# One-core MetaFormer kernel: three pairs of adder units summed on VectorE, a ring of six, and mixers, quantising and key table moved

## What is computed

```
x = x + relu(bn(adder2d_3x3(conv_3x3(relu(bn(adder2d_1x1(conv_1x1(ln(x)))))))) + ln(x))
t = t + routed(ln(t))      # 33 blocks; each takes op = argmax(h[0,0,:19]), and by two mask
                           # tables (33 x 19) for that op runs attention, a feed-forward, both or none
x = x + quantised_conv_relu x 2 (ln(x))
t = t + spectral(ln(t))    # 16 filters over the 784 tokens, mixed by 32x32 matrices
```

```
for kh in range(K):
    for kw in range(K):
        xs = xp[:, :, kh:kh + Ho, kw:kw + Wo]
        diff = jnp.abs(xs[:, None] - w[None, :, :, kh, kw, None, None])
        acc = acc - diff.sum(axis=2)          # over 32 input channels
```

## Time and profile before

| | us |
|---|---|
| runs | 362.1, 360.65, 361.57 (median 361.57) |
| profiled execution: time | 364.84 |
| profiled execution: span | 363.0 |
| PE busy in the span | 346.6 (95%) |
| DVE busy | 218.1 (60%) |
| ACT busy | 178.9 (49%) |
| POOL busy | 22.6 (6%) |
| adder 2 (first unit to last matmul) | 39.4 to 138.4 |
| first choice out | 148.2 |
| last stage | 259.8 to 359.7 |

### The profile page before, as it was taken

One profiled execution on the slowest core, in us unless ns is written; L12 is line 12 of the kernel. 1 busy time (PEld: TensorE's weight loads), 2 busy tenths in 40 slices (PEclk: granted clock), 3 DMA queues, 4 the chain that ended last, 5 costly groups with the idle time before them and its releaser, 6 DMA issues.

```text
span 363.0 us, 10721 instructions
## 1 busy us (share of the span) xinstructions
PE 346.6 (95%) x4689; PEld 208.2 (57%) x4689; DVE 218.1 (60%) x337; ACT 178.9 (49%) x182; POOL 22.6 (6%) x48
## 2 busy tenths in 40 slices
PE   8899999999999999899999998698999999999996
PEld 7436447744333335655673343384767777787873
DVE  2698999999999995454934795346422221111112
ACT  2871997878887952264827774503211111111111
POOL 5483000000000002000000000000000000000000
PEclk9999999999999999999969999969999999999999
DMA  5602800000000005400000000000140000000001
GB/s 172 223 21 57 326 13 2 2 3 2 2 2 0 2 2 206 165 5 15 1 2 2 1 3 2 7 0 0 29 110 4 4 2 4 2 4 4 2 4 46
DMA packets 12238, 13.13 MB, mean 36 GB/s; under 512 B 6027, under 2 KB 10909, under 8 KB 12185
## 3 DMA queue, kind: packets, MB, share of 16 engines
q1 hardware_dynamic: 11208, 9.17, 8.4%
q0 software_dynamic: 832, 3.00, 2.4%
q10 hardware_dynamic: 144, 0.20, 0.2%
HBM read 10.73 MB, written 0.40 MB: 31 GB/s over the span
## 4 chain that ended last, share of the span: by engine, by line
PE 64%; DVE 25%; issue 3%; ACT 2%; DMA 1%; SPq 0%; DVEq 0%; ACTq 0%
PE PS L1025 64%; DVE pool_ L848 17%; DVE pool_ L665 1%; DMA W1R<-in_fwa 1%; DVE pool_ L958 1%; DVE pool_ L845 1%; DVE pool_ L662 1%; ACT TMP L433 1%; DVE RSC L619 0%; DVE CW L783 0%; DVE CW L786 0%; DVE X L862 0%; DVE TMP L860 0%; DVE H L734 0%; DVE H L738 0%
## 5 line engine op out<-in xcount | busy, mean ns | idle before, releaser
L1025 PE MATMUL PS<-pool_,CON 128*32 128x392 f32 (+2 forms) x1320 | 111.4, 493 | 0.7 <-ACT pool_ L516 0.2
L1025 PEld LDWEIGHTS PS<-pool_,CON 128*32 128x32 f32 (+1 forms) x1320 | 48.9, 110 | 60.9 <-issue 43.8
L464 ACT ACTIVATE pool_<-TMP,WA 128x3136 f32<-128x3136 f32 x26 | 75.4, 2926 | 11.0 <-PE PS L1025 10.8
L848 DVE TENSOR_SCALAR pool_<-TMP,WA 128x3136 f32<-128x3136 f32 x44 | 79.4, 1844 | 0.1
L1003 DVE COPY pool_<-PS 128x392 f32<-128x392 f32 x32 | 18.1, 566 | 77.6 <-PE PS L1025 77.6
L565 ACT ACTIVATE pool_<-PS 128x392 f32<-128x392 f32 x32 | 15.9, 498 | 78.0 <-PE PS L1025 78.0
L1025 PE MATMUL PS<-HE,WS 128*32 128x392 f32 (+2 forms) x768 | 44.6, 386 | 0.2 <-ACT WS L557 0.2
L1025 PE MATMUL PS<-pool_,WS 128*32 128x392 f32 (+2 forms) x768 | 44.6, 385 | 0.0
L1025 PEld LDWEIGHTS PS<-pool_,WS 128*32 128x32 f32 x768 | 31.3, 109 | 12.2 <-issue 4.6
L1025 PEld LDWEIGHTS PS<-HE,WS 128*32 128x32 f32 x768 | 31.0, 110 | 12.8 <-issue 5.6
L1025 PE MATMUL PS<-CON 128*128 128x196 f32 (+1 forms) x142 | 29.9, 354 | 0.5 <-DVE QZ L652 0.5
(11 more groups left out here) (247 smaller groups left out, 334.7 us busy)
## 6 DMA issues: line engine op xcount, KB each, us to landing
pool_<-in_pho SPq DMA_DIRECT2D x1, 3144.0 KB, 11.8
HE<-in_phe SPq DMA_DIRECT2D x1, 3136.0 KB, 11.6
QZ<-CW SPq DMA_DIRECT2D x12, 98.0 KB, 2.2
CW<-in_cw POOLq DMA_DIRECT2D x2, 576.0 KB, 4.8
CON<-in_con POOLq DMA_DIRECT2D x1, 732.5 KB, 5.0
out_y<-Y SPq DMA_DIRECT2D x1, 392.0 KB, 2.4
CQ<-in_ws SPq DMA_DIRECT2D x16, 9.0 KB
MPP<-in_mpp POOLq DMA_DIRECT2D x1, 256.0 KB, 3.0
```

The source lines that it names most:

```text
L464: a.activation(unit, window(n // CQ), ACT.Abs, bias=WA2[:, n:n + 1], scale=-1.0).then_inc(s["act_unit"], 1)
L848: v.tensor_scalar(unit, window(n // CQ), WA2[:, n:n + 1], None, ALU.max).then_inc(s["dve_unit"], 1)
L1025: return t.matmul(out_, lhsT, rhs, start=start, stop=stop, skip_group_check=True)
```

## The change

- Adder 2: for c8 = 7 the units of taps (0, 1), (3, 4) and (6, 7) are summed on DVE before PE sees them: one max pass, a wait on it, then four `scalar_tensor_tensor` passes (max, add), one for each image. The pair stands in the second tap's place, the first tap's unit is gone: 69 groups instead of 72.
- The ring of adder 2 has six slots; the sixth is `QZ`, which adder 1 read and which is free by then.
- The mask tables are loaded as 19 partitions x 33. The key table is made on these (n = 16) and one DMA from SP lays it onto one partition.
- The quantising of both weights and the eight bias ops go to POOL, behind `decided`, as a chain in which each op waits for the one before: eight passes over 128 x 1152 and eight over 128 x 2. `cq_done` now comes from POOL, and the clear of `UPZ` follows it.
- `mixers(0, ...)` steps 4 and 5 move into the adder (n = 10, 12). All six of `mixers(1, ...)` move on DVE to just behind `decide(1)`. `u_mixers` move into the last stage (u = 25 to 31), and ACT's three `MUL` copies to u = 38.
- `widest`, `scales` and `box` change their n (24; 39; 20, 35, 50, 63).

```diff
 RG = 5
+RG2 = 6
+PAIRED = CQ - 1
+PAIRS = ((0, 1), (3, 4), (6, 7))
+FIRST_OF = {second: first for first, second in PAIRS}
+GROUPS = [((0,), c8) for c8 in range(CQ)]
+GROUPS += [((FIRST_OF[tap], tap) if c8 == PAIRED and tap in FIRST_OF else (tap,), c8)
+           for tap in range(9) for c8 in range(CQ) if not (c8 == PAIRED and tap in FIRST_OF.values())]
+NG = len(GROUPS)
+        def slot(g):
+            n = g % RG if g < CQ else (g - CQ) % RG2
+            return RING[:, n, :, :] if n < RG else QZ[:, :, :]
...
+            g.wait_ge(s["decided"], 1)
+            g.wait_ge(s["q_sc"], 1)
+            for src, dst, i in ((CW1, CQ1, 0), (CW2, CQ2, 1)):
+                gl(g.tensor_scalar(src[:, :], src[:, :], QS[:, 2 + i:3 + i], 1.0, ALU.mult, ALU.mult))
+                gl(g.tensor_scalar(src[:, :], src[:, :], 127.0, -128.0, ALU.min, ALU.max))
+                gl(g.tensor_scalar(src[:, :], src[:, :], 1.0, MAGIC, ALU.mult, ALU.add))
...
+                g.tensor_scalar(dst[:, :], src[:, :], -MAGIC, 1.0, ALU.add, ALU.mult).then_inc(s["cq_done"], 1)
             g.wait_ge(s["cq_done"], 2)
             g.memset(UPZ, 0.0).then_inc(s["zeroed"], 1)
...
-            for step in range(6):
+            for step in range(4):
                 mixers(0, step)
...
+                    elif len(taps) == 1:
+                        v.tensor_scalar(unit, window(taps[0]), WA2[:, at[0]:at[0] + 1], None, ALU.max).then_inc(s["dve_unit"], 1)
                     else:
-                        v.tensor_scalar(unit, window(n // CQ), WA2[:, n:n + 1], None, ALU.max).then_inc(s["dve_unit"], 1)
+                        v.tensor_scalar(unit, window(taps[0]), WA2[:, at[0]:at[0] + 1], None, ALU.max).then_inc(s["pair_half"], 1)
+                        v.wait_ge(s["pair_half"], PAIRS.index(taps) + 1)
+                        for b in range(NIMG):
+                            last = v.scalar_tensor_tensor(unit[:, b], window(taps[1])[:, b], WA2[:, at[1]:at[1] + 1], unit[:, b], ALU.max, ALU.add)
+                        last.then_inc(s["dve_unit"], 1)
...
             decide(1)
+            for step in range(6):
+                mixers(1, step)
```

More of the change, by code:

```diff
@@ L68 @@
 RG = 5
+RG2 = 6
 CQ = 8
-NG = CQ + 9 * CQ
-ON_ACT = [on_scalar(g % CQ) for g in range(NG)]
+PAIRED = CQ - 1
[5 more added lines that the diff above has]
+NG = len(GROUPS)
+ON_ACT = [on_scalar(c8) for taps, c8 in GROUPS]
 ACT_UPTO = [sum(ON_ACT[:g]) for g in range(NG + 1)]
@@ L439, in _ @@
             a.wait_ge(s["w_a_in"], 64)
-            for n in range(9 * CQ):
+            for n in range(NG - CQ):
                 g = CQ + n
+                (tap, *_), c8 = GROUPS[g]
                 if n == CQ:
@@ L445, in _ @@
                         a.activation(rows(S2P, h, 1, 1), grid(bank(4 + h)), ACT.Copy).then_inc(s["s2_ready"], 1)
[L446 to L454, removed]
                 if ON_ACT[g]:
-                    a.wait_ge(s["ring_free"], g - RG + 1)
-                    unit = RING[:, g % RG, :, :].rearrange("p b (r c) -> p b r c", r=SIDE)
+                    if n >= RG2:
+                        a.wait_ge(s["ring_free"], g - RG2 + 1)
+                    unit = slot(g).rearrange("p b (r c) -> p b r c", r=SIDE)
+                    bias = WA2[:, CQ * tap + c8:CQ * tap + c8 + 1]
                     if n == 1:
@@ L565, in _ @@
                 a.activation(UEV[:, u % 8, :], bank(u % 6), ACT.Copy).then_inc(s["uev_act"], 1)
+                if u == 38:
+                    a.wait_ge(s["u_mixed"], 4)
+                    for lag in range(3):
+                        q = slice(32 * lag, 32 * lag + 32)
+                        a.activation(MUL[q, :, :], MUS[q, :, C * lag:C * lag + C], ACT.Copy).then_inc(s["d_ready"], 1)
                 if u == 42:
@@ L776, in u_mixers @@
                                            ALU.mult, ALU.add).then_inc(s["u_mixed"], 1)
[L778 to L796, removed]
             nk = 0
@@ L804, in kl, with key_table @@
                 v.wait_ge(s["key_chain"], nk)
-            for step in range(6):
+            def key_table():
+                v.wait_ge(s["mask_in"], 32)
+                kl(v.tensor_copy(AMF[:, :], AMT[:, :]))
+                kl(v.scalar_tensor_tensor(KEY0[:, :], FMT[:, :], 2.0, AMF[:, :], ALU.mult, ALU.add))
+                kl(v.tensor_scalar(AMF[:, :], KEY0[:, :], 0.0, None, ALU.is_gt))
+                kl(v.tensor_tensor(AMF[:, :], AMF[:, :], con_("blk4", NB, NOPS), ALU.mult))
+                v.tensor_tensor(KEY0[:, :], KEY0[:, :], AMF[:, :], ALU.add).then_inc(s["key_made"], 1)
+            for step in range(4):
                 mixers(0, step)
@@ L815, in _ @@
             v.wait_ge(s["w_a_in"], 64)
-            for n in range(9 * CQ):
+            for n in range(NG - CQ):
                 g = CQ + n
-                if n == 20:
+                if n in (10, 12):
+                    mixers(0, 4 + (n - 10) // 2)
+                if n == 16:
+                    key_table()
+                if n == 24:
                     widest()
-                if n == 32:
+                if n == 39:
                     scales()
[L822 to L838, removed]
-                if not ON_ACT[g]:
-                    v.wait_ge(s["ring_free"], g - RG + 1)
-                    unit = RING[:, g % RG, :, :].rearrange("p b (r c) -> p b r c", r=SIDE)
+                if n in (20, 35, 50, 63):
+                    box((20, 35, 50, 63).index(n))
+                if not ON_ACT[g]:
+                    taps, c8 = GROUPS[g]
+                    at = [CQ * tap + c8 for tap in taps]
+                    if n >= RG2:
+                        v.wait_ge(s["ring_free"], g - RG2 + 1)
+                    unit = slot(g).rearrange("p b (r c) -> p b r c", r=SIDE)
                     if n == 0:
@@ L1117, in group @@
                     for b in range(NIMG):
-                        last = mm(PS[32 * b:32 * b + 32, 6 + h, 0:HT], SEL[ON_ACT[g]][:, g % CQ, :], half(RING[:, g % RG, b, :], h), fresh, False)
+                        last = mm(PS[32 * b:32 * b + 32, 6 + h, 0:HT], SEL[ON_ACT[g]][:, GROUPS[g][1], :], half(slot(g)[:, b, :], h), fresh, False)
                         if final and 4 * h + b < 7:
```

50 lines of the change are left out of this document (32 added, 18 removed).

## The result

The changed kernel takes 370.75 us (median of 4 runs, 368.77 to 371.19) against 361.84 for the kernel before (4 runs, 360.65 to 364.01). The ratio is 1.0229, 95% interval 1.0167 to 1.029: 2.3% slower, or 6 to 10.5 us. The forecast was 369.6. The profiled execution took 370.74, span 368.8. The profiled execution of the kernel before (span 363.0) lay 3 us above its median, so stages are compared here by landmarks and not by spans.

What follows compares the result with a forecast made beforehand. PE's pace was taken to set adder 2, with DVE only just keeping up. Adder -2.5, undisturbed mixers +0.5, taking turns +8.0 and clock +2.0 sum to +8.0 on the 361.57 median: 369.6 us, range 360.0 to 374.0.

Steps and rivals of the forecast that it cites:

- Adder, -2.5: Adder 2: three dropped groups save PE 3.95 us, less 1.5 of added waits behind the pairs, so 2.5 us gained.
- that case: Adder 2: with scalar_tensor_tensor passes of 0.97 us instead of 0.88, the stage gains only 1.5 us.
- The third pair: Adder 2, n=60: DVE was to end this pair 1.1 us before PE needs it.
- Moved and costed at nothing: Lag-weight copies and u mixers in the last stage, key table's DMA on SP: all said to fit, cost zero.
- Mixers undisturbed, +0.5: DVE behind the choice: 3.1 us of mixers against 2.5 of slack make the first feed-forward unit 0.5 us late.
- Taking turns, +8.0: Behind the choice: DVE's mixers and GpSimd's passes exclude each other on SBUF, seven holds of 1.15 us, 8.0 us.
- the rival that they pass freely: Behind the choice: DVE's two-input ops pass GpSimd, only L763 collides (0.9); total -1.1 us, 360.5; chance 0.30.
- forecast 8.5: Choice to DVE's first hidden unit: forecast to lengthen by 8.5 us, for undisturbed mixers (0.5) and taking turns (8.0).
- Clock, +2.0: Behind PE's idle stretch before the attention: granted clock falls to 0.50, costing 2.0 us, between 0 and 3.5.
- UPZ: GpSimd behind its chain: with passes of 1.2 us, UPZ is cleared a little before the attention asks at 164.68.
- The 0.18 for a faster kernel: Chance that the change is faster: the part of the rival with DVE's two-input ops passing GpSimd that lies below 359.8.

Runs made afterwards that it cites:

- no_pairs: Changed kernel with no tap pairs in adder 2 (72 groups), all else as changed: 372.21 us, ratio 1.0284 to the kernel before.
- chain_later: Changed kernel with GpSimd's chain started behind the fourth hidden unit of DVE and the attention's wait on zeroed lowered to 3: 365.77 us, ratio 1.0104.
- repaired: Changed kernel with pairs at (2,3), (5,6), (7,8), GpSimd's chain started behind DVE's fourth hidden unit, second mixers in the last stage: 359.01 us, ratio 0.9899.
- chain_writes_only: Changed kernel with GpSimd's eight long passes replaced by memsets of the same size, weights' quantising left out: 364.52 us, one run.
- the fillers: Changed kernel with 40 filler matmuls of 98 columns on PE in the idle gap of the first feed-forward step: 374.05 us, ratio 1.0359.
- mixers_late: Changed kernel with the six second-set mixer steps moved from behind the choice to behind the second residual sum: 363.5 us, ratio 1.0029.
- pairs_spaced: Changed kernel with taps paired (2,3), (5,6), (7,8) in place of (0,1), (3,4), (6,7): 367.59 us, ratio 1.0171.

## Why the prediction was right, and where only its sum was

The direction and the size came out (+8.0 forecast, +8.9 measured), and so did the mechanism that carried 8.0 of the forecast and 5.5 of the measured time. Two steps were off by nearly 3 us each, in opposite directions, and that they cancel is luck.

**Adder, -2.5; measured -1.52.** The mis-sized term is the pass of scalar_tensor_tensor. I took 0.88, by taking off the overlap that whole units show; it is 0.97, as its length alone says. The text gave -1.5 for that case. Against the kernel before, waits took 2.4 of the 3.95 where I had 1.5 (1.8 against 0.3); against no_pairs the pairs' own waits are 2.8. The third pair, which I had ending 1.1 early, left no lead either: PE waits for a unit behind it, with a box step of 0.97 in between.

**Moved and costed at nothing.** Right for ACT's lag-weight copies (0.96 at 323.77; the next eviction still waits 2.00 for PE), for the u mixers (the last stage is as long as before), for SP's wait and for the key table's DMA.

**Mixers undisturbed, +0.5; measured +3.3.** This step failed. I read the idle 2.14 ahead of the copy of B2C as a wait for W2S, and hence as slack for work put in front. In the kernel before, W2S did land last, 0.2 us ahead of the copy. In the changed code the idle time isn't slack. In chain_later W2S had been issued 1.1 us earlier than before and had landed by 153.6, the mixers came first, the look-ahead ended at 153.71, and the gap behind it was 3.51. It starts behind the look-ahead, however late that is. How long it would have been in the kernel before with W2S already there, no run shows. Of the 3.3 the mixers make 2.8 (10.27 in chain_later, 7.46 in repaired, which has neither mixers nor passes there); the other 0.5 is lost without them too (7.46 against 6.97).

**Taking turns, +8.0; measured +5.12 (mixers) and +0.33 (look-ahead).** That they exclude each other was right, for two-input ops too, and the rival that they pass freely fell with chain_writes_only. The size failed in its counting. Held ops of L802 take 1.20 instead of 0.35, so a hold costs 0.85. Beside them GpSimd's passes follow at 1.23 from start to start (151.38 to 155.07), one for each DVE op, and the op's own 0.35 lies inside that time; I had added the whole pass to it. At 0.85 each the 5.12 are six holds for eight ops, and not seven: three on L802, one on L799, and two (1.77) on the four ops of L797.

**Together**: 3.3 + 5.12 + 0.33, less 0.84 for an issue gap of 0.96 ahead of PINT that falls to 0.12 when the mixers take longer, is 7.91; the traces have +7.87 for the forecast 8.5.

**Clock, +2.0; measured +1.56** between the two traces and 1.43 by the fillers. The level (0.50 until 166) was as forecast.

**UPZ.** GpSimd's passes took 1.15 to 1.27 but for the first (forecast 1.2), the clear ended at 161.23 (forecast 161.5), and the attention didn't wait.

**Chances.** The 0.18 for a faster kernel rested on two-input ops passing GpSimd. By the Trainium skill ("SBUF — State Buffer", Who interferes with whom), which I had weighed, it deserved less.

## What to carry to other kernels

Idle time ahead of an instruction that is the first behind a jump need not be slack, even where a DMA lands last: here it moved along with the work put in front of it. Elementwise work put on two engines at once is not parallel if it meets on SBUF; ask for each op of VectorE whether it has two SBUF inputs while GpSimd reads. Where a freed engine leads by nothing, the place of a long instruction decides more than its number: three pairs at other taps gained 2.0 us more with the same work.

## What was not expected of the hardware

- Ahead of its first instruction behind the jump VectorE stood idle for 3.35 to 4.04 us in the changed kernel and nine variants, with nothing that ends it in the trace. In the three kernels where W2S landed last it was 2.14, 2.28 and 2.83, and the jump can have taken that long at most. The Trainium skill ("Advanced Engine Details and Errata", Control Flow Timing) gives about 108 ns for a compare-and-branch; no run here shows a jump of this length for so little.
- The granted clock may fall, or not, in the same code. In the 11 us ahead of the attention's 56 matmuls of W4R and H, PE is busy without a gap at 1.00 in the kernel before (172.68 to 183.65) and in mixers_late (173.59 to 184.53). Behind them before's trace has these levels (columns as above):

```profile
184.00:187.00 3.00, 3.00 (x57) 2.76 (x54) 0.79 (x4) 0.92 (x1) 0.00 (x0) 0.63 0.00 0
187.00:190.00 3.00, 3.00 (x19) 2.16 (x22) 0.51 (x1) 0.54 (x1) 0.00 (x0) 0.50 0.00 0
```

  while mixers_late keeps 1.00 from 185 to 195. From these 56 matmuls to PE's first of TMP and W4R before takes 37.79, the changed kernel 37.06, repaired 36.65, and mixers_late, chain_later and pairs_spaced 35.43. That is 2.4 us between executions with no difference in that code, more than most effects looked for here.
